# A ternary feed-forward kernel on one core: order of the gate loads, small matmuls at the start, the last aggregation in quarters, and a new split of the gate sums

## What is computed

```
h = gelu(cond @ W0 + b0);  h = gelu(h @ W1 + b1)
att = softmax(h @ W2 + b2)                      # 64 x 8
agg_w = einsum('bk,koi->boi', att, weight)      # 64 x 64 x 64
agg_b = att @ bias_k
y = einsum('boi,bih->boh', agg_w, x) + agg_b[:, :, None]
scale = mean(abs(w));  q = round(clip(w / (scale + 1e-5), -1, 1));  deq = q * scale
inter = (y @ deq_gate.T) * (y @ deq_up.T)       # 2752 columns
out = x + inter @ deq_down.T
```

## Time and profile before

| | us |
|---|---|
| median of 3 runs | 1734.46 |
| lowest and highest | 1733.05, 1734.97 |
| the profiled execution | 1734.24 |
| its span | 1732.4 |
| PE busy in the span | 1705.4 (98%) |
| DVE, ACT busy | 1097.0 (63%), 576.4 (33%) |

### The profile page before, as it was taken

One profiled execution on the slowest core, in us unless ns is written; L12 is line 12 of the kernel. 1 busy time (PEld: TensorE's weight loads), 2 busy tenths in 40 slices (PEclk: granted clock), 3 DMA queues, 4 the chain that ended last, 5 costly groups with the idle time before them and its releaser, 6 DMA issues.

```text
span 1732.4 us, 31273 instructions
## 1 busy us (share of the span) xinstructions
PE 1705.4 (98%) x12380; PEld 1209.9 (70%) x12388; DVE 1097.0 (63%) x1785; ACT 576.4 (33%) x921; POOL 29.2 (2%) x57
## 2 busy tenths in 40 slices
PE   5999999999999999999999999999999999999999
PEld 3454555977769596795958868597776958678584
DVE  5888896555765458554685546855576555855464
ACT  6777742312333133231333213231233313333120
POOL 0010001000000000000000000000000000000000
PEclk8999999999999999999999999999999999999999
DMA  9656725412232121410224121331223312132021
GB/s 341 248 199 236 252 93 190 148 46 97 75 123 101 41 107 65 180 65 22 107 95 170 65 75 54 121 142 45 97 75 111 112 43 107 65 123 74 31 90 49
DMA packets 59687, 194.06 MB, mean 112 GB/s; under 512 B 5264, under 2 KB 5712, under 8 KB 59536
## 3 DMA queue, kind: packets, MB, share of 16 engines
q1 hardware_dynamic: 56464, 177.62, 28.9%
q0 software_dynamic: 2480, 14.22, 2.2%
q10 hardware_dynamic: 592, 0.09, 0.0%
HBM read 160.90 MB, written 31.01 MB: 111 GB/s over the span
## 4 chain that ended last, share of the span: by engine, by line
PE 96%; SPq 1%; DMA 1%; DVE 1%; ACT 1%; issue 0%; DVEq 0%
PE ps L877 52%; PE ps L934 24%; PE ps L657 16%; PE ps L895 2%; SPq L526 1%; DMA wuT<-in_L_ffn_w_gate_dram 1%; PE ps L757 1%; ACT aT L261 0%; DVE msk L1438 0%; DVE xa L1509 0%; DVE prod L1476 0%; ACT wdT L1092 0%; SPq L490 0%; DVE xa L1512 0%; ACT wgT L1108 0%
## 5 line engine op out<-in xcount | busy, mean ns | idle before, releaser
L877 PE MATMUL ps<-yp,wgT 128*128 128x256 f16 x4116 | 902.6, 273 | 2.4 <-issue 2.2
L877 PE MATMUL ps<-wuT,wgT 128*128 128x256 f16 x4116 | 902.6, 273 | 0.0
L877 PEld LDWEIGHTS ps<-yp,wgT 128*128 128x128 fp8e4 x4116 | 402.9, 98 | 53.1 <-issue 5.3
L877 PEld LDWEIGHTS ps<-wuT,wgT 128*128 128x128 fp8e4 x4116 | 402.7, 98 | 48.3
L934 PE MATMUL ps<-wdT,inter 128*128 128x512 fp8e4 x1960 | 433.2, 379 | 0.0
L934 PEld LDWEIGHTS ps<-wdT,inter 128*128 128x128 f16 x1960 | 191.2, 98 | 227.0 <-issue 1.4
L1743 DVE SCALAR_TENSOR_TENSOR xr<-ps,osc,xr 128x512 f32<-128x512 f32 x210 | 156.6, 749 | 168.0 <-PE ps L934 128.4
L1692 DVE TENSOR_TENSOR wdT<-ps,msk 128x512 f32<-128x512 f32 (+1 forms) x77 | 51.3, 667 | 207.1 <-PE ps L877 207.1
L1221 ACT COPY raw<-ps 128x512 f32<-128x512 f32 (+1 forms) x77 | 43.6, 567 | 316.5 <-PE ps L877 315.9
L1228 ACT COPY msk<-ps 128x512 f32<-128x512 f32 (+1 forms) x77 | 43.6, 567 | 140.5 <-PE ps L877 140.5
L1243 ACT COPY inter<-ps 128x256 f32<-128x256 f32 x70 | 26.1, 372 | 180.1 <-PE ps L877 180.1
(11 more groups left out here) (224 smaller groups left out, 1488.6 us busy)
## 6 DMA issues: line engine op xcount, KB each, us to landing
wgT<-wcomb SPq DMA_DIRECT2D x70, 896.0 KB, 4.7
wdT<-dcomb SPq DMA_DIRECT2D x14, 2240.0 KB, 10.4
xa<-in_x_dram SPq DMA_DIRECT2D x8, 2048.0 KB, 7.9
out_dram<-xr SPq DMA_DIRECT2D x64, 256.0 KB, 2.0
wcomb<-xa POOLq DMA_DIRECT2D x17, 448.0 KB, 3.6
xr<-in_L_ffn_w_down_dram SPq DMA_DIRECT2D x9, 512.0 KB, 5.6
inter<-in_L_ffn_w_gate_dram SPq DMA_DIRECT2D x7, 512.0 KB, 16.1
wdT<-in_L_ffn_w_up_dram SPq DMA_DIRECT2D x7, 512.0 KB, 4.2
```

The source lines that it names most:

```text
L877: last = nc.tensor.matmul(out, w, operand(i, OPERAND[what])[:, k, :], start=(start and h + k + i == 0), stop=(k == KQ - 1 and i == 1), ski ...
```

## The change

It makes these edits. The gate tile of 64 rows is loaded third, behind tiles 0 and 1 and `x`, instead of last. `bias_k` and `wk_in` are loaded ahead of tile 0 instead of behind it. Four f32 matmuls of 128 x 128 on data that nobody reads run on PE between the logits and the transpose of the attention weights. DVE sums the positions 2, 6, 13, 15, 17 and 18 (with the 64-row tile in position 2) instead of 5, 10, 12, 15 and 19, and ACT the rest; sums, scalings, casts and subtractions are put in a new order on both engines. On PE seven of the eight 448-column matmuls of the later aggregation stand ahead of `total(0)`, in two portions with a wait for ACT's sums ahead of each, and the eighth is cut into four of 112 columns that stand between `total(0)`, the two halves of the transposes and the first group.

```diff
-    loads += [(n, True, True, s) for n, s in enumerate(wd + base + it + wu)]
+    gate = [(n, True, True, s) for n, s in enumerate(wd + base + it + wu)]
+    loads += gate[:2] + gate[FT:] + gate[2:FT]
...
-    SUM_DVE, HALVES = (5, 10, 12, 15, 19), (NG - 2, NG - 1)
+    SUM_DVE, HALVES = (2, 6, 13, 15, 17, 18), (NG - 2, NG - 1)
...
+            sp.dma_start(biask[:, :], bias_k).then_inc(s_cond3, 16)
+            sp.dma_start(wk_in, wk.rearrange("k (a g) i z -> (k a) g (i z)", g=OG)).then_inc(s_cond3, 16)
...
             mm(ps[3][0:B, 0:NK], h2, w2_sb).then_inc(s_pe, 1)
+            for _ in range(4):
+                mm(YB[1][:, 0:P], ones[:, :], ident)
...
-                for e in halves:
-                    last = mm(agg_bank(a, g)[e * C:(e + 1) * C], wk_in[:, g, :], attd[:, e, :, t0:t1])
-                if e:
+                for e, i, n in pieces:
+                    cols = slice(i * (t1 - t0) // n, (i + 1) * (t1 - t0) // n)
+                    last = mm(agg_bank(a, g)[e * C:(e + 1) * C, :, cols], wk_in[:, g, :], attd[:, e, :, t0:t1][:, :, cols])
+                if (e, i) == (1, n - 1):
                     last.then_inc(s_agg, 1)
...
-            for g in range(OG - 1):
-                pe.wait_ge(s_sum_act, sum(on_act[:NG - 5 + g]))
-                agg_w(1, g, (0, 1))
+            pe.wait_ge(s_sum_act, sum(on_act[:NG - 5]))
+            agg_w(1, 0)
+            agg_w(1, 1)
+            pe.wait_ge(s_sum_act, sum(on_act[:NG - 2]))
+            agg_w(1, 2)
+            agg_w(1, 3, ((0, 0, 1),))
             total(0)
-            agg_w(1, OG - 1, (0,))
-            for h in range(2):
-                transpose_first(h)
-            agg_w(1, OG - 1, (1,))
+            agg_w(1, 3, ((1, 0, 4), (1, 1, 4)))
+            transpose_first(0)
+            agg_w(1, 3, ((1, 2, 4),))
+            transpose_first(1)
+            agg_w(1, 3, ((1, 3, 4),))
...
-            after = {0: (2,), 3: (3,), 4: (4,), 7: (6, 7, 8, 9, 11, 13)}
+            after = {1: (3,), 3: (4,), 5: (5,), 7: (7, 8, 9)}
...
             for k in range(KH):
                 conv(0, k)
-            raw_sum(5)
+                if k == 3:
+                    raw_sum(2)
+            raw_sum(6)
```

More of the change, by code:

```diff
@@ L507, in _ @@
             for e, (n, _, _, s) in enumerate(loads):
[L508 to L511, removed]
+                if e == 2:
                     load_x(0)
@@ L677, in _, with agg_w @@
             pe.wait_ge(s_cv, 9)
-            def agg_w(a, g, halves):
+            def agg_w(a, g, pieces=((0, 0, 1), (1, 0, 1))):
                 t0, t1 = AGG[a]
@@ L686, in agg_w @@
                         pe.wait_ge(s_yv, KH - 1)
-                for e in halves:
-                    last = mm(agg_bank(a, g)[e * C:(e + 1) * C], wk_in[:, g, :], attd[:, e, :, t0:t1])
-                if e:
+                for e, i, n in pieces:
+                    cols = slice(i * (t1 - t0) // n, (i + 1) * (t1 - t0) // n)
+                    last = mm(agg_bank(a, g)[e * C:(e + 1) * C, :, cols], wk_in[:, g, :], attd[:, e, :, t0:t1][:, :, cols])
+                if (e, i) == (1, n - 1):
                     last.then_inc(s_agg, 1)
             for g in range(OG):
-                agg_w(0, g, (0, 1))
+                agg_w(0, g)
             pe.wait_ge(s_bsel, 2)
@@ L1115, in _ @@
                     raw_sum(i)
-            for n in range(2):
+            hi_y(0)
+            for i in (10, 11):
+                raw_sum(i)
+            hi_y(1)
+            for i in (12, 14):
+                raw_sum(i)
+            for n in (2, 3):
                 hi_y(n)
-            for i in (14, 16, 17, 18):
+            raw_sum(16)
+            hi_y(4)
+            for i in (19, *HALVES):
                 raw_sum(i)
[L1120 to L1124, removed]
+            for n in (5, 6):
                 hi_y(n)
@@ L1517, in _ @@
                 conv(0, k)
-            raw_sum(5)
+                if k == 3:
+                    raw_sum(2)
+            raw_sum(6)
             scales(0)
-            for n in range(3):
+            for n in range(6):
                 scale_y(0, FIRST_K[n])
[L1522 to L1525, removed]
-            out_scales(0)
[L1527 to L1533, removed]
+            raw_sum(13)
+            scale_y(0, FIRST_K[6])
+            raw_sum(15)
+            split_y(0)
+            raw_sum(17)
+            split_y(1)
+            raw_sum(18)
+            split_y(2)
+            scale_y(0, FIRST_K[7])
+            out_scales(0)
             for i in HALVES:
@@ L1536, in _ @@
             partition_sums(0, ND)
-            split_y(2)
             threshold(0)
```

## The result

The changed kernel takes 1740.68 us (median of 6 runs, 1738.82 to 1741.31) against 1734.12 of the kernel before (6 runs, 1733.05 to 1734.97). The ratio is 1.0033, 95% interval 1.0023 to 1.0044: 5.7 us slower by the ratio (4.0 to 7.6), 6.6 by the medians. The forecast was 1733.4, and its range of 1731.6 to 1735.5 does not hold the result. The profiled execution took 1739.17 us, its span is 1737.4: 5.0 us longer than the span before.

What follows compares the result with a forecast made beforehand. PE bounds the kernel; only its 20 idle us ahead of 51.5 us can be won. Gains of 0.25 and 0.8 make 1.05 us, from 1734.24 to 1733.2; the median lies 0.2 above: 1733.4, range 1731.6 to 1735.5.

Steps and rivals of the forecast that it cites:

- The step that failed: Start, ahead of 51.5 us: only PE's 20 idle us there can be won, and what is won is kept.
- The four small matmuls: Softmax, between logits and transpose: they end at 9.1 us, which costs nothing; the wait for `x` hides some tenths.
- (c): Aggregation quarters: short runs cost as much as a whole half, 1.7 us each, `copy_first` 3.1 later: 1737.1; chance 0.07.
- rival (b): Start: cheaper slow stretch or earlier clock, landing 41.2, `tot` 42.0, all slots done, - 2.0 us: 1732.2; chance 0.15.
- the main line: Start: `total(0)` 0.25 us earlier and `copy_first` 0.8 sooner behind it, 1732.8 to 1733.9; chance 0.45.
- The landing: Last gate tile's transfer: lands at 41.8 us (41.2 to 42.3) instead of 42.31, with the 64-row tile third.
- the slow stretch: Transfers at 37.0 to 41.5 us: 228 GB/s instead of 408, from the 64-row tile; moves to around 14, cost 1.7.
- `x` late by 0.9 us: Convolution start on PE: the moved slow stretch reaches the tail of `x` and delays it 0 to 2.0 us, taken 0.9.
- `total(0)`: PE's add of `tot` over partitions: behind seven aggregation halves, at 43.1 us instead of 43.35, 0.25 earlier.
- From `total(0)` to the end of `copy_first`: Start: quarters instead of a 1.74 us half ahead of the transposes, + 2.6 to + 2.9 instead of + 3.50; gain 0.8.

Runs made afterwards that it cites:

- with 16 matmuls: The changed kernel without the four small f32 matmuls in the softmax, no padding: 1735.90 us, ratio 1.0011 to the kernel before.
- the run of the load order alone: The kernel before with only the new order of loads, old sums and aggregation, and 40 idle one-column matmuls ahead of the loop: 1730.37 us, ratio 0.9980.
- the run with the tile last: The changed kernel with the 64-row tile loaded last again and 26 idle one-column matmuls ahead of the loop: 1730.72 us, ratio 0.9981.
- the run with 40: The kernel before with 40 one-column matmuls on unread data behind the norms of chunk 0: 1732.20 us, ratio 0.9988.
- before + 14: The kernel before with 14 one-column matmuls on unread data behind the norms of chunk 0: 1739.19 us, ratio 1.0029.

## Why the prediction was wrong

**The step that failed** is in its first paragraph: "what is won there is kept, since the groups that follow are chained to one another by PE alone". That PE is busy from 51.5 us on says that no other engine holds it up. It does not say that its own instructions are there in time. The chunk loop jumps back four times, and each jump costs the time until the next block of instructions is there, less the work that stands in the first block. Added instructions were priced only at the place at which they run ("The four small matmuls": "which costs nothing"), and no term asked what they do to the place of the code behind them. The size of the missing term is + 6.8 us in the profiled execution (1687.7 - 1680.9), about 1.3 us a pass and 1.7 of clock once. None of the rivals had it; (c), the slower one, named the quarters for another reason. And (c) at its own price, 1737.1, lay outside the range that was said to hold all cases but the extremes. What the prediction did foresee, a start that comes earlier, is there, and more of it than forecast: rival (b), not the main line, is what came (landing at 41.1, `tot` at 41.90, the slots done), and 1.85 us of its 2.0.

**What covers the wait.** From the first matmul of a pass to the end of the second gap it is 1.03 + 2.04 = 3.1 us in the pass shown of the changed kernel, 1.91 + 0.95 = 2.9 with 16 matmuls, and 2.56 + 0.43 = 3.0 before. Over all 20 passes with a gap it is 2.5 to 3.4 us, with a mean of 2.9, and it does not follow the number of matmuls in front of the gap. So the next block arrives about 3 us into the pass whatever is done, and only the work in front of it differs: the gap is 1.4 to 2.0 us behind 8 or 9 matmuls, 0.7 to 1.5 behind 16 and 0.04 to 0.7 behind 22. In the four passes in which the instruction transfer started 0.84 us or more behind the first matmul, and not 0.15 to 0.29, it is 3.1 to 3.4 us. The Trainium skill, page Runtime: NRT & Kernel Launch, section "Instruction fetch mechanics", also says that a taken branch to code outside the current two blocks forces a fetch of the target before work goes on. The short first gap, 0.06 to 0.33 us in all kernels, may be what is left of that here; no run separates the two fetches. Nor does one tell how much of the wait is owed to the other transfers that run at the start of a pass.

**The landing (41.8 forecast, 0.3 to 0.5 earlier).** The mechanism was right, the size too small: 41.08, 1.2 us earlier. The term that was mis-sized is the cost of the slow stretch at its new place, 0.8 us instead of 1.7. The estimate of 0.7 us that the prediction made from the Trainium skill, SBUF — State Buffer, section "Door 1: The DMA port swizzle", fits this place and not the other two (2.0 and 1.4). With the tile last in the changed order of work it is about 1.3 (289 GB/s over 4.5 us, above). What makes those longer is open.

**`x` late by 0.9 us.** Wrong: PE's convolution starts at 14.27, before at 14.30. In the profiles of all kernels it starts between 13.7 and 14.9, and the three latest are kernels with the old order.

**`total(0)`.** Forecast 43.1, measured 42.13. It stood behind the aggregation, as in the paragraph on it; the halves were done at 42.1 because their start came at 36.41 and not at 37.9 (`x` was not late, and the convolution was sooner done, since PE's clock rose at 17.3 us and not at 19.8). PE's clock rose at 41.2.

**From `total(0)` to the end of `copy_first`.** Forecast + 2.6 to 2.9 us, measured 43.81 + 1.18 - 42.13 = 2.86. The size is right, and quarters of 0.2 to 0.43 us came as 0.62 for two and 0.43 for one. Rival (c), which would have made the non-contiguous pieces dear, is refused by these rows. What the Trainium skill says of such patterns (PSUM — Partial Sum Buffer, section "Specifications (TRN2)") does not show in a time here. But the mechanism, that the interval shrinks because the 1.74 us half is cleared from it, is not borne out. The run without quarters, with the last half whole behind the transposes, takes 2.76 us. And the run of the load order alone, which has the old order with a whole half between `total(0)` and the transposes, takes 43.62 + 1.10 - 41.91 = 2.81:

```profile
42.22 0.96 PE L657 MATMUL ps<-inter 128*64 128x448 f32 x2
...
43.62 1.10 ACT L1111 ACTIVATE wgT<-ps 128x512 fp8e4<-128x512 fp8e4 x2 [0.48 <-PE ps L767]
```

Its clock was still at 1.00 there, so that the half took 0.96 us and not 1.74, and the transposes waited for DVE. In the three kernels with padding and the old order of loads, whose clock was at 0.50, the interval is 3.7 us. So what shortens the interval is the clock at that moment. The seven profiles with the new order of work (2.76 to 2.87 us) all have it at 1.00 there; what taking the half away is worth at 0.50 no run shows.

**The four small matmuls.** "They end at 9.1": at 9.40. The transpose behind them started 0.12 us later than before (9.33 for 9.21), and that was made up by 10.42. That they bring the clock up earlier, as part of (b) said, is not shown: 32 matmuls of the convolution take 5.49 us in the changed kernel and 6.67 before, but in the run with the tile last, which has the four too, they take

```profile
13.87 6.55 PE L656 MATMUL ps<-ablk,xa 128*128 128x128 f32 x32 [0.28 <-DMA xa<-in_x_dram]
```

The clock rises at 17.2 to 20.4 us in the four kernels profiled with them and at 18.4 to 19.8 in the eight without. At the end they are worth nothing (1730.38 without them, 1730.50 with).

**The parts** do not add up. The prediction summed a gain from the loads and one from the order of work; the runs give 1.8 us for the loads alone, 1.5 for the rest alone, and 1.7 for both, all against the run with 40. The kernel with 40 has a granted clock of 0.5 for longer around 43 to 49 us in its profile than the kernel before, as have the other two padded kernels with the old order of loads, so part of the gap to it may be the clock's. Which share, the runs do not settle.

## What to carry to other kernels

Where an engine runs a hardware loop and is the bound, count the instructions that a change adds ahead of the loop on that engine, and look in the trace for a gap a fixed number of instructions into each repeated pass, with a transfer of the instruction queue ahead of its end. Padding in an idle stretch moves that gap, and tells within one run whether a small change is slow by itself or by the place that it gives the code behind it. Compare two versions of such a kernel with the loop at the same place in its block, or the comparison measures the place.

## What was not expected of the hardware

- A matmul kernel with PE busy for 98% of the span gained 2.3 us (1734.46 to 1732.20) from 40 matmuls that do nothing, and the changed kernel, at 1740.68, came to 1730.50 with 26 of them.
- A wait in the loop (2.04 and 1.66 us) was followed by a fall of PE's clock to 0.50 in one of four passes, in the profile of the changed kernel and in that of before + 14; each cost about 1.7 us. Other waits as long, up to 2.04 us, were not followed by one. In the other ten profiles no fall was seen between 50 us and the last us of the span.
- The same 64-row transfer loses 2.0 us of transfer time as the last of the gate tiles (1.3 in a second kernel) and 0.8 us as the third.
- The profile shows the fetches of a loop: a queue of kind "instruction" with one transfer of 16.4 KB for 256 instructions, and PE goes on 1.2 to 1.6 us behind the end of the one that it waits for.
